# Writing out the image loop of a deformable-convolution stage on four engines

## The reference, cut to what matters

```python
off = offset.reshape(b_, K, 2, h_, w_)                # K = 9 taps, offsets from a small convolution
py = off[:, :, 0] + rows + ky;  px = off[:, :, 1] + cols + kx
def corner(yi, xi, wt):                               # fetch the pixel of one corner, weighted
    g = jax.vmap(lambda im, yy, xx: im[:, yy, xx])(x, yc, xc)
    return g * (wt * valid)[:, None]
p = corner(y0i, x0i, ...) + corner(y0i, x0i + 1, ...) + corner(y0i + 1, x0i, ...) + corner(y0i + 1, x0i + 1, ...)
out = jnp.einsum('bckhw,ock->bohw', p, w.reshape(co, c_, K))
x = x + gelu(batch_norm(out + b))
```

## Time and profile before

| What | us |
|---|---|
| Median of 3 runs | 3529.34 |
| Lowest and highest of the 3 runs | 3527.95, 3532.04 |
| The profiled execution, its own time | 3531.29 |
| Its span, from the first to the last instruction | 3529.4 |
| Of that: the pass over the images (first gather to last product) | about 167 to 1440 |
| Batch norm and GELU | about 1440 to 1590 |
| Block attention | about 1590 to 2270 |
| Head attention | about 2270 to 3529 |

### The profile page before, as it was taken

How to read it: one execution, slowest core, us unless ns; L and a number is a source line. 1 busy time by engine, 2 the same in 40 slices (tenths; PEclk the granted TensorE clock), 3 DMA queues, 4 the chain that set the end, 5 groups by cost and what they waited for, 6 DMA issues and landing times. The chain is left out here.

```text
span 3529.4 us, 64576 instructions
## 1 busy us (share of the span) xinstructions
PE 3229.3 (91%) x20030; PEld 2274.4 (64%) x20030; DVE 2692.8 (76%) x5130; ACT 2439.1 (69%) x5999; POOL 1468.7 (42%) x1536
## 2 busy tenths in 40 slices
PE   7989999999999999769999999968988989888887
PEld 3468878787787888658888888734444444444443
DVE  4588889888888988668888888736777677677775
ACT  4456666666666666647777777728878778777784
POOL 2245545454444555432222222221255454453535
PEclk9999999999999999889999999968999999999997
DMA  7699999999999999720000000022223222322221
GB/s 284 237 386 388 387 365 392 354 389 359 383 374 352 382 362 381 277 75 16 18 18 16 18 16 18 18 77 66 58 82 94 64 79 67 92 74 67 57 71 51
DMA packets 216833, 640.97 MB, mean 182 GB/s; under 512 B 31232, under 2 KB 111104, under 8 KB 216192
## 3 DMA queue, kind: packets, MB, share of 16 engines
q0 software_dynamic: 82944, 453.02, 33.3%
q1 hardware_dynamic: 133632, 184.79, 16.3%
HBM read 529.65 MB, written 62.62 MB: 168 GB/s over the span
## 5 line engine op out<-in xcount | busy, mean ns | idle before, releaser
L2062 DVE TENSOR_REDUCE e_neg_top<-e_next 128x1 f32<-128x1024 f32 x384 | 469.7, 1224 | 196.0 <-PE e_next L2375 168.3
L519 DVE SCALAR_TENSOR_TENSOR b_mix<-b_got,b_weight,b_mix 128x384 f32<-128x384 f32 x864 | 528.1, 618 | 89.3 <-ACT b_mix L603 47.6
L519 DVE SCALAR_TENSOR_TENSOR b_mix<-shared,b_weight,b_mix 128x384 f32<-128x384 f32 x864 | 528.5, 618 | 80.2 <-ACT b_mix L603 58.6
L615 ACT ACTIVATE b_s_high<-b_bank 128x384 fp32r<-128x384 f32 x576 | 283.7, 493 | 405.8 <-PE b_bank L725 405.8
L2229 ACT ACTIVATE e_prob<-e_s 128x512 f32<-128x512 f32 x768 | 416.6, 598 | 126.2 <-PE e_s L2387 124.8
L2214 ACT ACTIVATE e_unused<-e_next,e_neg_top 128x1024 bf16<-128x1024 f32 x384 | 430.5, 1121 | 102.4 <-DVE e_neg_top L2062 102.4
L402 POOL DMA_INDIRECT b_got<-pair_table,b_index x288 | 309.2, 1074 | 320.2 <-DVE b_mix L519 248.3
L402 POOL DMA_INDIRECT shared<-pair_table,b_index x288 | 307.4, 1067 | 310.9 <-DVE b_mix L519 243.5
L1282 ACT ACTIVATE d_w_qkv<-d_back,d_neg_top 128x128 f32<-128x128 f32 x768 | 269.7, 392 | 143.4 <-DVE d_neg_top L1185 143.4
L748 PE MATMUL b_bank<-b_s_high,b_w_high 128*128 128x512 f32 x1296 | 357.2, 403 | 0.0
L748 PE MATMUL b_bank<-b_s_high,b_w_low 128*128 128x512 f32 x1296 | 348.7, 395 | 0.0
(11 more groups left out here) (243 smaller groups left out, 6449.8 us busy)
## 6 DMA issues: line engine op xcount, KB each, us to landing
pair_table<-kept SPq DMA_DIRECT2D x16, 1536.0 KB, 13.3
e_stack<-e_high SPq DMA_DIRECT2D x384, 64.0 KB, 2.0
shared<-in_x SPq DMA_DIRECT2D x8, 1536.0 KB, 7.6
shared<-in_x SPq DMA_DIRECT2D x16, 768.0 KB, 12.2
tokens<-y SPq DMA_DIRECT2D x64, 192.0 KB, 1.9
e_tok<-tokens SPq DMA_DIRECT2D x8, 1536.0 KB, 7.5
e_stack<-e_low SPq DMA_DIRECT2D x192, 64.0 KB, 2.0
shared<-tokens SPq DMA_DIRECT2D x8, 1536.0 KB, 7.2
```

Of the source, the lines that this page charges most:

```text
L519: ins = nc.vector.scalar_tensor_tensor(dst[:], src[:, q * C:(q + 1) * C], weight[g][:, q, k, i:i + 1], dst[:], ALU.mult, ALU.add)
L615: nc.scalar.activation(here(s_high, s, i), tps[t % 2][:, 0:C].rearrange("p (o q) -> p o q", q=P), ACT.Copy).then_inc(highs_made, 1)
L2062: nc.vector.reduce_max(neg_top[s % 2][:, t:t + 1], b_next[t % 2][:], AX.X, negate=True).then_inc(top_ready, 1)
```

## The change

The hardware loops over the images of this stage are replaced by loops of the program that writes the code. All four engines now have eight copies of the image's instructions one behind the other. There is no register for `n`, no compare-and-branch, and every wait is for a constant. What is computed, and in which order, stays as it was on every engine. The semaphore `counted` is gone; DVE's statistics count on in `fchain`, which stood at 64 at the end of the first part, and ACT waits for 64 plus the old number. The address of a statistics slot is a constant instead of one computed from a register.

```diff
@@ gpsimd
-                with pool.Fori(1, BATCH) as n:
+                for n in range(1, BATCH):
                     gather(n)
@@ vector
-                    ins = nc.vector.bn_stats(conv_stats[:, o, bass.ds(2 * n + g, 1)], src[:, o])
+                    ins = nc.vector.bn_stats(conv_stats[:, o, 2 * n + g:2 * n + g + 1], src[:, o])
                     if o == CH - 1:
-                        ins.then_inc(counted, 1)
+                        ins.then_inc(fchain, 1)
...
-                with dve.Fori(1, SPILLED) as n:
-                    blends(n)
-                blends(SPILLED, this=False)
-                for n in range(SPILLED + 1, BATCH):
-                    blends(n, before=False, this=False)
+                for n in range(1, BATCH):
+                    blends(n, before=(n <= SPILLED), this=(n < SPILLED))
@@ scalar
-                        act.wait_ge(counted, 2 * n + g)
+                        act.wait_ge(fchain, 8 * BATCH + 2 * n + g)
...
-                with act.Fori(1, SPILLED) as n:
-                    turn(n)
-                turn(SPILLED, this=False)
-                for n in range(SPILLED + 1, BATCH):
-                    turn(n, is_last=(n == LAST), before=False, this=False)
+                for n in range(1, BATCH):
+                    turn(n, is_last=(n == LAST), before=(n <= SPILLED), this=(n < SPILLED))
@@ tensor
-                with pe.Fori(1, BATCH) as n:
+                for n in range(1, BATCH):
                     turn(n)
```

More of the change, by code:

```diff
@@ L274, in offsets_and_conv @@
         acc_ready = sem("b_acc_ready")
-        counted = sem("b_counted")
         y_staged = sem("b_y_staged")
@@ L627, in take @@
                     act.wait_ge(acc_ready, 2 * n + g + 1)
-                    if spilled and not (isinstance(n, int) and n == 0 and g == 0):
+                    if spilled and not (n == 0 and g == 0):
                         act.wait_ge(y_spilled, 32 * n + 16 * g)
-                        act.wait_ge(counted, 2 * n + g)
+                        act.wait_ge(fchain, 8 * BATCH + 2 * n + g)
                     dst = staged if spilled else kept[:, 2 * (n - SPILLED) + g]
@@ L739, in product @@
                     g, k = divmod(s, TAPS)
-                    if i == 0 and k == 0 and not (isinstance(n, int) and n == 0):
+                    if i == 0 and k == 0 and not (n == 0):
                         pe.wait_ge(y_staged, 2 * n + g - 1)
```

## The result

| | Median, us | Lowest to highest | Against before, with its 95% interval |
|---|---|---|---|
| Before | 3530.69 | 3527.95 to 3535.22 (4 runs) | 1 |
| Changed | 3491.93 | 3490.18 to 3495.07 (4 runs) | 0.989 (0.9873 to 0.9907) |

The changed kernel is 1.1% faster. Its profiled execution took 3492.49 us with a span of 3490.7, which is 38.7 us less than the span of before. The forecast was 3492.3 us.

The account below looks back on a forecast made before the run. PE was taken to set the pace in the pass over the images, losing time at taken back edges. Edges 37.0 us, constants 0 and longer code 0, off 3529.34, gave 3492.3 us; 8-in-10 range 3487 to 3505 us.

Parts of the forecast that it names:

- What bounds the stage: Pass over the images: PE sets the pace at 150.57 us an image without edges; DMA engines can keep giving 390 GB/s.
- The rival in which the gathers set the pace: Pass over the images: DMA cannot sustain more, ACT would wait for gathers; no change, about 3529 us; chance 0.04.
- The back edges: Image loop: six stretches with a taken edge fall from 940.42 to 903.42 us, gain 37.0 us; chance 0.84.
- waits on constants: Register instructions between matmuls and DVE's steps go: at most 0.45 us for seven images, taken as 0.
- the two counts that bounded it: Six image edges: 24.4 us of array idle time alone, or 38.1 us with half of the 27.3 us at half clock.
- The forecast of the median: Whole kernel: 3529.34 - 37.0 = 3492.3 us, 1.05% faster.
- DVE's and ACT's stops lie in the same moments and are not added: Image changes: DVE's and ACT's own stalls of 20 us each coincide with PE's, so they add nothing.
- Longer code: Pass over the images: each engine streams new code instead of repeating one body; taken as 0.
- Block attention's loops: Loops at L1079, at new addresses, might be brought in again on 29 edges: 174 us slower, 3666 us; slower cases 0.05.
- The branches cost next to nothing: Image loop: six edges worth 0.063 us each, 0.4 us in all, idle time stays; 3529 us; chance 0.01.

Follow-up runs that it names:

- pairs kernel: Changed kernel with PE's images 1 to 6 as a loop over three pairs, image 7 written out: 3505.21 us, again 3504.91 us.

## Why the prediction was right, point by point

- *What bounds the stage.* Right: PE's pace in the images set it, and DMA had room. The six stretches after run at 379 to 390 GB/s, where those of before had 365 to 377, and ACT waits for no gather. The rival in which the gathers set the pace is out.
- *The back edges, 37.0 us.* Right: the six stretches gave 37.9 us, of which 0.9 us belongs to the waits on constants below. The term for the edges was taken as whole stretches with and without an edge, and PE's loop alone brought 36.4 us back. The cause given for it, code that has to be brought in, is borne out by the packets of q8 inside the long branches, one or two of 16 KB in each of the six. Behind each edge the clock had stood at 0.50 for 3.4 or 6.8 us. Of the two counts that bounded it, the 24.4 us of idle time was far too low, so the clock's share came back with the idle time. The upper one, 38.1 us, counted some idle time twice: of the 27.3 us at half clock PE was busy for 24.47, and half of that gives 36.6 us.
- *The forecast of the median.* That it came within 0.4 us is in part luck: 37.0 us were taken off a median of 3529.34 us, and with a fourth run that median is 3530.69, so that the gain by medians is 38.8 us.
- *DVE's and ACT's stops lie in the same moments and are not added.* Right for the sum, and shown: alone they cost 15.0 and 18.6 us, together with PE's the total is 38.8. What the text did not say is that they would have become the next bound, had only PE been written out.
- *Waits on constants, 0 with a bound of 0.45 us.* Too small. The stretch without an edge went from 150.57 to 150.43 us, 0.14 us an image or 1.0 us in seven. It is PE's own: in the pairs kernel, whose ACT and DVE are written out, the looped images take 150.57 us and the written-out last one 150.44. The bound came from 56 tiles inside an image, which hold one of the two moments of an image at which PE's array waits for its sums. In the first stretch it stands idle there for 0.38 and 0.39 us before, and for 0.30 us both times after, and the window saw only one of the two. That the matmuls already queued hide all of the register instructions was the author's estimate; 0.14 us an image was not hidden.
- *Longer code, 0.* Right: every stretch is alike and the branch that was left out did not come back as another wait. That the long body was brought in anew on every turn already, the trace of before shows: from 500 to 640 us, inside image 2 and away from its edges, q8 brings 6 packets, and between 490 and 632 us the changed kernel's straight code takes 6 as well. The number of instruction packets even fell, from 129 to 112 on the queue q8, about three for each edge; what code those three carried, the trace does not say.
- *Block attention's loops.* They kept their price in their new place: PE's branch there is 0.208 us in the median as before, and from 1555 to 2235 us only the queue q1 is at work, with no instruction packet. The boundaries across which a body might come to lie were the author's assumption; no run shows one.

```profile
L1072 PEldq COMPARE_BRANCH  x30: 76/208/238, 1552.3 to 2224.1; - x30
q1 hardware_dynamic: 8496, 11.60, 4.7%
```

- *The branches cost next to nothing.* Out: the six edges gave 37.9 us and not 0.4. The record of a branch is 0.063 us at most on DVE and up to 0.223 us on PE to code that was just executed, but 4.3 to 7.9 us on PE to the top of a body of an image.

## What to carry to other kernels

Cut a loop into stretches of equal work, one of them without a back edge; their difference is the price of an edge on the path, with the clock's share in it, and it needs no theory of the cause. A hardware loop was dear here where its code was brought in again on every turn, and then on every engine that has such a loop and feeds the bound one; write out all of these, since their stops fall together and any one left over keeps its own. Counted in the trace of before from one branch to the next, the bodies with stops have 1718 instructions on PE, 449 on DVE and 411 on ACT; those without have 219 on POOL and, in block attention, 449 on PE. So these short loops could stay, but one length does not hold for all engines, and from which length on an engine stops was not measured. The packets of the instruction queues told which case it was: against the code written out, q8 had 17 more with PE's loop over the images, and q14 11 and 16 more with ACT's and DVE's; but q14 had 7 fewer with POOL's, and q8 had 50 fewer with the loops of block attention.

## What the runs showed of the hardware that was not expected

- At the image loop the record of the branch holds the stop on PE (4.3 to 7.9 us) and not on ACT and DVE, where the branch is 0.045 and 0.063 us at most and the stop stands as idle time by issue in front of the next instruction (up to 6.2 us).
- PE's clock fell at the stops of ACT or DVE alone too: with ACT's loop the stretches with an edge have 0.99. With DVE's the stretch in front of an image change has 1.00 and the next 0.99, as with PE's own edges (0.98 or 0.99); of that next one, 480 to 488 us has 1.00, and 490 to 500 us, where PE stood idle, 0.83.

```profile
325.67:476.07 150.40, 35.36 (x216) 1.00 0.99 391
476.07:631.11 155.04, 35.77 (x216) 0.99 0.97 378
```

- Two edges of the same loop cost different amounts: 5.2 and 2.3 us in one execution of the pairs kernel, where the second stop was 4.5 us long and the granted clock stayed at 1.00 behind it, and 5.4 and 5.3 us in the other. The first execution's two stretches:

```profile
626.86:782.60 155.74, 35.79 (x216) 0.99 0.98 376
933.18:1086.07 152.89, 35.44 (x216) 1.00 0.98 382
```
